# Row sums of x2 on VectorE ahead of the product with ones, and new orders of the later begin and of the end, in a four-layer conditioned residual block

## The reference

```python
# layer 0: a weight of rank 30 per entry, decoded from cond_512
U = (mu @ W_dec + b_dec).reshape(B, 257, 30); param = einsum('bik,kj->bij', U, V)
x = x + x @ param[:, :-1] + param[:, -1]
# layer 1: style-modulated product, demodulated, plus bias, clipped to +-256
x = x + clip(dcoef * ((x * style) @ weight) + bias, -256, 256)
# layer 2: down to 64 features, relu, up again, both conditioned on the entry
w_down = down_project * dg + db; w_up = up_project * ug + ub
x = x + relu(x @ w_down) @ w_up + x
# layer 3: layer norms with gains by token, three small nets on the conditions,
#          all weighted by softmax(aw), into a net 1536 -> 256 -> 256 with a last layer norm
x = x + _mlp_ln(concat([w0*h, w1*t, w2*m, w3*n, w4*r, w5*s]), int_W1, ..., int_g, int_be)
```

## Time and profile before

| | |
|---|---|
| median of 3 runs | 518.64 us (517.88, 518.64, 521.16) |
| span of the profiled execution | 518.5 us |
| the profiled execution's own time beside its span | none shown; the run nearest to the span is 518.64 |
| PE busy | 486.3 us (94%) |
| DVE busy | 410.5 us (79%) |
| ACT busy | 355.5 us (69%) |
| POOL busy | 406.9 us (78%) |
| mean granted TensorE clock | 0.985 |

### The profile page before, as it was taken

One profiled execution on the slowest core, in us unless ns is written; L12 is line 12 of the kernel. 1 busy time (PEld: TensorE's weight loads), 2 busy tenths in 40 slices (PEclk: granted clock), 3 DMA queues, 4 the chain that ended last, 5 costly groups with the idle time before them and its releaser, 6 DMA issues.

```text
span 518.5 us, 9615 instructions
## 1 busy us (share of the span) xinstructions
PE 486.3 (94%) x3216; PEld 361.9 (70%) x3245; DVE 410.5 (79%) x701; ACT 355.5 (69%) x666; POOL 406.9 (78%) x380
## 2 busy tenths in 40 slices
PE   8987788999999999999999999999999999988993
PEld 4854555677777686868686877777777767677782
DVE  4978697668788788788888888788888788887753
ACT  4677657558667677776878777777777776657732
POOL 6737798988798979798988888888989788786501
PEclk9999699999999999999999999999999999999997
DMA  8994507324234261708080817162534425113102
GB/s 294 336 335 98 127 1 219 82 82 127 83 89 120 60 189 36 212 21 226 0 236 11 214 33 195 53 176 72 139 110 118 133 54 148 53 40 125 41 2 80
DMA packets 35117, 61.82 MB, mean 119 GB/s; under 512 B 5107, under 2 KB 17541, under 8 KB 34708
## 3 DMA queue, kind: packets, MB, share of 16 engines
q1 hardware_dynamic: 28788, 44.01, 30.4%
q0 software_dynamic: 5440, 16.87, 11.0%
q10 hardware_dynamic: 864, 0.61, 0.4%
HBM read 52.61 MB, written 8.87 MB: 119 GB/s over the span
## 4 chain that ended last, share of the span: by engine, by line
PE 75%; ACT 7%; DVE 6%; issue 5%; POOL 5%; DMA 1%; DVEq 0%; ACTq 0%; POOLq 0%
PE ps_d L966 10%; PE ps_c L916 9%; PE ps_c L918 9%; PE ps_c L917 9%; PE ps_d L980 5%; PE ps_a L994 4%; PE ps_b L916 3%; PE ps_b L917 3%; PE ps_b L918 3%; PE ps_b L1012 3%; PE ps_a L1006 2%; POOL pw_rows L1532 2%; PE ps_a L1012 2%; DMA set_wdec<-in_W_dec 1%; PE ps_b L935 1%
## 5 line engine op out<-in xcount | busy, mean ns | idle before, releaser
L1232 ACT ACTIVATE h<-h,nb_h,rstd_h 128x256 f32<-128x256 f32 x64 | 33.3, 591 | 41.2 <-POOL nb_h L1562 41.2
L966 PE MATMUL ps_d<-xm_t,l_w 128*128 128x512 f32 x128 | 59.8, 610 | 1.7 <-DVE h L1455 0.9
L1532 POOL DMA_INDIRECT pw_rows<-in_pw,gidx x40 | 39.0, 976 | 12.2 <-issue 12.2
L1577 POOL TENSOR_TENSOR h<-xhat,pw_rows 128x1024 f32<-128x1024 f32 x16 | 38.0, 2374 | 6.4 <-ACT xhat L1232 6.4
L966 PEld LDWEIGHTS ps_d<-xm_t,l_w 128*128 128x128 f32 x128 | 23.6, 194 | 26.7 <-issue 24.5
L1596 POOL TENSOR_TENSOR w_up<-up_rep,ugub 128x1024 f32<-128x1024 f32 x16 | 38.1, 2378 | 2.9 <-DMA ugub<-ugub_scratch 1.9
L1598 POOL TENSOR_TENSOR w_up<-w_up,ugub 128x1024 f32<-128x1024 f32 x16 | 39.3, 2456 | 1.3
L1582 POOL TENSOR_TENSOR h<-h,pw_rows 128x1024 f32<-128x1024 f32 x16 | 38.3, 2396 | 1.2
L994 PE MATMUL ps_a<-act_dn,w_up 128*128 128x128 f32 x256 | 33.4, 286 | 5.3 <-ACT act_dn L1211 4.7
L1608 POOL TENSOR_TENSOR x3be<-x,ln_gb 128x1024 f32<-128x1024 f32 x16 | 37.9, 2372 | 0.3 <-DVE y_out L1513 0.3
L916 PE MATMUL ps_b<-w_h,act_t_l 128*128 128x256 f32 x128 | 37.7, 295 | 0.4 <-DVE act_t_l L1477 0.4
(11 more groups left out here) (263 smaller groups left out, 1607.9 us busy)
## 6 DMA issues: line engine op xcount, KB each, us to landing
ugub<-ugub_scratch SPq DMA_DIRECT2D x32, 512.0 KB, 6.6
x_t<-in_x_t SPq DMA_DIRECT2D x16, 512.0 KB, 6.5
out<-y_out SPq DMA_DIRECT2D x15, 512.0 KB, 7.2
set_wdec<-in_W_dec SPq DMA_DIRECT2D x2, 1920.0 KB, 9.6
set_wdec<-in_int_W SPq DMA_DIRECT2D x1, 1536.0 KB, 11.1
set_wdec<-in_nets_rows SPq DMA_DIRECT2D x1, 1152.0 KB, 15.5
set_wdec<-in_nets_W SPq DMA_DIRECT2D x1, 768.0 KB, 6.5
pw_rows<-in_pw,gidx POOLq DMA_INDIRECT x40, 3.6
```

The source lines that it names most:

```text
L966: m = eng.matmul(ps_l1[:, o, :], l1_w[:, k, o * P:(o + 1) * P], xm_t[:, k, :], start=k == 0, stop=k == KB - 1)
L1232: m = eng.activation(out[:, j, :], src[:, j, :], ACT.Identity, bias=nb[k][:, j:j + 1], scale=rstd[k][:, j:j + 1])
L1532: eng.indirect_dma_start(pw_rows[:, j, :], None, t["pw"], bass.IndirectOffsetOnAxis(ap=idx[:, j:j + 1], axis=0)).then_inc(s_pw[c.ring], 16)
L1577: eng.tensor_tensor(h1[:, :, :], xhat[:, :, :], pw_rows[:, :, 0:D], ALU.mult).then_inc(g_h1m, 1)
```

## The change

A tile x2_sum (128 x 512 float32) and a VectorE stage `v_xsum` are added. `v_xsum` adds the two feature halves of x2, right after `v_x2add` in each list, for all 16 chunks. `pe_dn` takes part 0 from x2 as before (four matmuls) and part 1 from x2_sum with one half of the ones (two matmuls instead of four), after a wait for `v_xsum`. The loop's orders stay as they are, with `v_xsum` put in. The semaphore d_aw is merged into d_bias (load_aw moves ahead of load_side, and the waits for d_bias become 32), and `act_onehot` waits for its own previous one-hot. The lists of the later begin and of the end are written anew on each engine.

```diff
@@ pe_dn
             x = x2_t[c.ring][:, :, :].rearrange("p k (j e s) -> p k e j s", e=2, s=S)
-            for part in range(2):
-                for k in range(KB):
-                    for e in range(2):
-                        m = eng.matmul(ps_dn[e * HID:(e + 1) * HID, part * CT * S:(part + 1) * CT * S],
-                                       down_w[:, k, part * HID:(part + 1) * HID], x[:, k, e],
-                                       start=k == 0, stop=k == KB - 1)
+            for k in range(KB):
+                for e in range(2):
+                    eng.matmul(ps_dn[e * HID:(e + 1) * HID, 0:CT * S], down_w[:, k, 0:HID], x[:, k, e],
+                               start=k == 0, stop=k == KB - 1)
+            wait(eng, v_xs, c.n + 1)
+            x = x2_sum[:, :].rearrange("p (j e s) -> p e j s", e=2, s=S)
+            for e in range(2):
+                m = eng.matmul(ps_dn[e * HID:(e + 1) * HID, CT * S:2 * CT * S], down_w[:, 0, HID:P], x[:, e],
+                               start=True, stop=True)
             m.then_inc(p_dn, 1)
@@ act_onehot
             wait(eng, s_idx[c.ring], 32 * (c.half + 1))
+            wait(eng, a_oh, c.n)
@@
+        def v_xsum(eng, c):
+
+            if first(c):
+                eng.wait_ge(d_ug, 16)
+            wait(eng, v_x2, c.n + 1)
+            wait(eng, p_dn, c.n)
+            eng.tensor_tensor(x2_sum[:, :], x2_t[c.ring][:, 0, :], x2_t[c.ring][:, 1, :], ALU.add).then_inc(v_xs, 1)
@@ TensorE, begin
-                             (pe_dn, 0), (pe_t, 2), (pe_warm, 2), (pe_up, 0), (pe_x3r, 0), (pe_l1, 1),
-                             (pe_x1, 2), (pe_mot, 0), (pe_xht, 0), (pe_cls, 0), (pe_dn, 1), (pe_row, 0),
-                             (pe_t, 3), (pe_cp, 0), (pe_up, 1), (pe_warm, 3), (pe_warm, 4), (pe_x3r, 1),
+                             (pe_t, 1), (pe_hid, 0), (pe_l1, 0), (pe_mo, 0), (pe_x1, 1), (pe_dn, 0), (pe_t, 2),
+                             (pe_warm, 2), (pe_up, 0), (pe_l1, 1), (pe_x3r, 0), (pe_mot, 0), (pe_x1, 2), (pe_cls, 0),
+                             (pe_xht, 0), (pe_dn, 1), (pe_row, 0), (pe_t, 3), (pe_up, 1), (pe_cp, 0), (pe_warm, 3),
...
@@ ScalarE, begin
-                             (act_w1scale, 0), (act_u, 2), (act_onehot, 0), (act_relu, 0), (act_w1high, 0),
-                             (act_th1, 2), (act_th2, 2), (act_x3, 0), (act_onehot, 1), (act_xnorm, 0),
-                             (act_mot, 0), (act_u, 3), (act_xht, 0), (act_x3h, 0), (act_th1, 3), (act_relu, 1),
-                             (act_shift, 0), (act_hnorm, 0), (act_rowwrite, 0), (act_hh, 0), (act_th2, 3),
+                             (act_onehot, 0), (act_u, 3), (act_relu, 0), (act_onehot, 1), (act_th1, 2),
+                             (act_w1high, 0), (act_th2, 2), (act_x3, 0), (act_mot, 0), (act_xnorm, 0), (act_xht, 0),
+                             (act_x3h, 0), (act_relu, 1), (act_shift, 0), (act_hnorm, 0), (act_th1, 3),
...
@@ VectorE, begin
-                             (v_x2add, 0), (v_x1add, 1), (v_w1sum, 0), (v_dnmul, 0), (v_dnadd, 0),
-                             (v_mostat, 0), (v_x3sum, 0), (v_xstat, 0), (v_monorm, 0), (v_l1mul, 1),
+                             (v_l1mul, 0), (v_l1min, 0), (v_x2add, 0), (v_xsum, 0), (v_x1add, 1), (v_dnmul, 0),
+                             (v_mostat, 0), (v_dnadd, 0), (v_w1sum, 0), (v_x3sum, 0), (v_monorm, 0), (v_xstat, 0),
...
@@ VectorE, loop: the one difference
+                             (v_x2add, 3), (v_xsum, 3), (v_hlow, 5), (v_tmprod, 5), (v_dnmul, 3), (v_dnadd, 3),
...
@@ GpSimd, begin
-                             (g_dcoef, 0), (g_tlow, 1), (g_wup, 0), (g_style, 1), (g_moroot, 0), (g_w1tlow, 0),
-                             (g_tlow, 2), (g_w1xlow, 0), (g_rootx, 0), (g_w2low, 0), (g_w1mlow, 0), (g_hmul, 0),
-                             (g_hadd, 0), (g_wup, 1), (g_rooth, 0), (g_style, 2), (g_gather, 1), (g_res, 0),
+                             (g_dcoef, 0), (g_tlow, 1), (g_wup, 0), (g_w2low, 0), (g_style, 1), (g_moroot, 0),
+                             (g_wup, 1), (g_w1mlow, 0), (g_tlow, 2), (g_rootx, 0), (g_w1tlow, 0), (g_hmul, 0),
+                             (g_hadd, 0), (g_w1xlow, 0), (g_style, 2), (g_rooth, 0), (g_gather, 1), (g_res, 0),
...
@@ GpSimd, end
-                      end=[(g_wup, 13), (g_hmul, 12), (g_hadd, 12), (g_tlow, 14), (g_rooty, 10), (g_gather, 13),
-                           (g_rooth, 12), (g_res, 12), (g_style, 14), (g_rootx, 13), (g_wup, 14), (g_hmul, 13),
-                           (g_hadd, 13), (g_rooty, 11), (g_tlow, 15), (g_rooth, 13), (g_gather, 14),
+                      end=[(g_wup, 13), (g_hmul, 12), (g_hadd, 12), (g_tlow, 14), (g_rooty, 10), (g_res, 12),
+                           (g_rooth, 12), (g_style, 14), (g_gather, 13), (g_rootx, 13), (g_wup, 14), (g_hmul, 13),
+                           (g_hadd, 13), (g_tlow, 15), (g_rooty, 11), (g_rooth, 13), (g_gather, 14), (g_style, 15),
...
```

More of the change, by code:

```diff
@@ L274, in conditioned_residuals @@
         x2_t = x1_t
-        (d_front, d_bdec, d_aw, d_side, d_bias, d_l1, d_wts, d_id, d_net, d_w2n, d_rown, d_w1, d_late, d_oh, d_gain, d_cls,
+        x2_sum = late("x2_sum", [P, CH])
+        (d_front, d_bdec, d_side, d_bias, d_l1, d_wts, d_id, d_net, d_w2n, d_rown, d_w1, d_late, d_oh, d_gain, d_cls,
          d_ub, d_ug, d_row) = (
             sem("d_" + n) for n in
-            "front bdec aw side bias l1 wts id net w2n rown w1 late oh gain cls ub ug row".split())
+            "front bdec side bias l1 wts id net w2n rown w1 late oh gain cls ub ug row".split())
         d_dec = [sem(f"d_dec{n}") for n in range(KB)]
@@ L430, in load_aw @@
         def load_aw(eng, c):
-            eng.dma_start(aw[:, :], row(t["aw"]).broadcast_to([P, 6])).then_inc(d_aw, 16)
+            eng.dma_start(aw[:, :], row(t["aw"]).broadcast_to([P, 6])).then_inc(d_bias, 16)
         def load_side(eng, c):
@@ L608, in v_awmax @@
         def v_awmax(eng, c):
-            eng.wait_ge(d_aw, 16)
+            eng.wait_ge(d_bias, 32)
             v_link(eng.reduce_max(aw_c[0][:, :], aw[:, :], AX.X))
@@ L728, in act_style @@
             eng.wait_ge(m_st, 1)
-            eng.wait_ge(d_bias, 16)
+            eng.wait_ge(d_bias, 32)
             for o in range(KB):
@@ new lines, in _ @@
+                             (act_rowwrite, 0), (act_hh, 0), (act_x3, 1), (act_xnorm, 1), (act_th2, 3), (act_tmh, 0),
+                             (act_relu, 2), (act_gidx, 3), (act_msh, 0), (act_xht, 1), (act_x3h, 1), (act_u, 4),
+                             (act_hnorm, 1), (act_silu, 0), (act_silh, 0), (act_th1, 4), (act_x3, 2), (act_hh, 1),
+                             (act_xnorm, 2), (act_th2, 4), (act_tmh, 1), (act_relu, 3), (act_ysquare, 0),
+                             (act_msh, 1), (act_xht, 2), (act_onehot, 2), (act_x3h, 2)],
@@ new lines, in _ @@
+                             (v_l1mul, 0), (v_l1min, 0), (v_x2add, 0), (v_xsum, 0), (v_x1add, 1), (v_dnmul, 0),
+                             (v_mostat, 0), (v_dnadd, 0), (v_w1sum, 0), (v_x3sum, 0), (v_monorm, 0), (v_xstat, 0),
+                             (v_l1mul, 1), (v_l1min, 1), (v_x1add, 2), (v_x2add, 1), (v_xsum, 1), (v_classes, 0),
+                             (v_dnmul, 1), (v_dnadd, 1), (v_hstat, 0), (v_x3low, 0), (v_rows, 0), (v_x3sum, 1),
+                             (v_hprod, 0), (v_xstat, 1), (v_hlow, 0), (v_l1mul, 2), (v_l1min, 2), (v_x2add, 2),
@@ new lines, in _ @@
+                             (v_xsum, 2), (v_tmprod, 0), (v_dnmul, 2), (v_dnadd, 2), (v_tmlow, 0), (v_msprod, 0),
+                             (v_hstat, 1), (v_mslow, 0), (v_x3low, 1), (v_x3sum, 2)],
+                      order=[(v_x1add, 3), (v_hprod, 5), (v_xstat, 4), (v_sillow, 6), (v_l1mul, 3), (v_l1min, 3),
+                             (v_x2add, 3), (v_xsum, 3), (v_hlow, 5), (v_tmprod, 5), (v_dnmul, 3), (v_dnadd, 3),
+                             (v_tmlow, 5), (v_msprod, 5), (v_ygain, 6), (v_mslow, 5), (v_hstat, 4), (v_ynorm, 6),
+                             (v_x3low, 4), (v_x3sum, 3)],
```

160 lines of the change are left out of this document (69 added, 91 removed).

## The result

The changed kernel takes 525.71 us (median; 523.85 to 527.31) against 519.9 for the kernel before on the same chip: a ratio of 1.0113, with a 95% interval of 1.0077 to 1.015. It is slower by 1.1%. The profiled execution of it took 527.31 us at a span of 525.5, so its time lies 1.8 above its span. It is the slowest of the four runs: its mean granted clock is 0.978, theirs 0.981 to 0.984. The sum of the prediction set the span of 518.5 equal to a time, and so began about 1.5 us too low.

What follows compares the result with a forecast made beforehand. TensorE's own queue was taken to bound the loop. From 518.5 us, +4.8 for the sum, -2.0 for the begin and -2.3 for the end gave 519.0 us, with a range of 511.0 to 524.5.

Steps and rivals of the forecast that it cites:

- The bound of the loop: Loop: TensorE's own instructions set the 27.2 us period; v_hlow ends 1.0 us before pe_w2, all the room there is.
- Removed from TensorE: pe_dn: four matmuls fewer, 0.47 us per chunk, 7.5 us over 16 chunks if all of it counted.
- Added to VectorE: v_xsum in the loop: held until GpSimd's running w_up ends, plus 0.55; about 1.2 us instead of 0.69.
- What is queued behind it: Loop: v_hlow ends late, so pe_w2 does too; period 0.4 us longer, +4.8 us over 12 chunks.
- The begin and the end of the sum: v_xsum outside the loop: 0.69 us in the begin; 0.4 us for each of the end's first two chunks.
- The orders: New lists of begin and end: -2.0 us in the later begin, -2.3 us in the end.
- rival of the held clock: Begin: a shorter TensorE gap keeps the 2.4 GHz level, 2.7 us less, 516.3 us; chance 0.10.
- pe_l1(1) ahead of it: Begin: pe_l1(1) before pe_x3r(0) makes chunk 0 late, +3.0 instead of -2.0, 524.0 us; chance 0.17.
- a sum that nothing blocks: Loop: VectorE and GpSimd don't exclude each other, or GpSimd's phase slips clear; pe_w2 0.13 early, 512.6 us; chance 0.10.
- The full saving: Loop: all of the 0.47 us arrives because pe_w2 does not meet v_hlow's end, 508.6 us; chance 0.08.
- GpSimd keeping its turn: Loop: v_xsum waits for GpSimd's next instruction (L1577) too, +2.6 us in 12 chunks, 545 us; chance 0.04.

Runs made afterwards that it cites:

- e8: The changed kernel without v_xsum, with the short pe_dn: the ones product reads x2's first feature half alone; 513.42 us.
- e3: The changed kernel with one input of v_xsum taken from PSUM (ps_l1) and not from SBUF; 514.53 us.
- e12: The changed kernel with the sum and short pe_dn in the loop's ten chunks alone; 0.63% or 3.3 us above the new orders without the sum.
- e14: The changed kernel with the sum and short pe_dn in chunks 0 to 2 alone; 2.3 us above the new orders without the sum.
- e15: The changed kernel with the sum and short pe_dn in chunks 13 to 15 alone; 2.7 us above the new orders without the sum.
- e2: The changed kernel without v_xsum and with the old eight-matmul pe_dn, so the new orders alone; 515.6 us.
- e9: The changed kernel with v_xsum run but unused: pe_dn has its old eight matmuls and no wait for the sum; 522.94 us.
- e4: The changed kernel with GpSimd's second w_up instruction (128x1024) cut into four of 128x256; 525.31 us.

## Why the prediction was wrong

**The bound of the loop: right.** TensorE's queue, 1.0 us from v_hlow.

**Removed from TensorE: right in size.** e8 shows 0.43 of the 0.47.

**Added to VectorE: right for the loop.** The exclusion, its end 0.55 behind the running instruction and the cause (e3) held. I forecast v_xsum at about 1.2 us; it took 1.18 and 1.29.

**What is queued behind it: right.** I took +0.4 a period, from 27.2 to "near 27.6"; it is 0.32 to 0.33 (27.53 to 27.54). For the 12 chunks of that pattern that is 3.9 instead of 4.8, and e12 measured 3.3 us for ten of them.

**The begin and the end of the sum: this step failed.** The sum was priced at 0.69 in the begin ("v_xsum (0.69) and v_mostat (52.53 to 54.88, 2.35) in front"), and the end had 0.4 for each of its first two chunks and nothing for the last. The row from which I took the rule, 1.88 and 2.72 us for L685 and L686, was itself from the begin and said what a sum costs that meets a GpSimd instruction just begun. I used it for the loop's phase alone ("the ten chunks of the loop and the first two of the end"), where 0.65 us of the instruction were left. Six sums outside the loop stand in other phases: 1.94, 1.00 and 2.79 us in the begin and 1.37, 2.68 and 0.69 in the end. By e14 and e15 they cost 2.3 and 2.7 us, and on top of the loop's ten 6.7 (changed kernel against e12). In the profiled execution TensorE stood 1.74 and 1.31 us for two of them, and behind each wait its clock fell and took 1.5 us more, a term that my sum didn't have. The range should have held 16 sums, each between 0.69 and 2.95 us (2.4 and 0.55).

**The orders: the size right, half of the causes wrong.** I took -2.0 and -2.3, 4.3 together; the spans of e2 and the kernel before differ by 4.3 and the ratios by 0.79%, 4.1 us. The halves are 1.3 in the begin and 3.0 in the end, by the traces. In the begin pe_up(0) takes 2.02 us at 53.10 in e2 (3.75 at 53.62 before): the clock stayed at its upper level behind a gap of 2.15 us instead of 3.34, which was my rival of the held clock. pe_x3r(0) still starts at 58.43 (58.77 before), so pe_l1(1) ahead of it cost nothing and its rival was wrong. Nor did it gain: in the changed kernel pe_up(0) stands at 53.47 and not near 52, behind a wait of 0.87 us for the sum of chunk 0, and pe_x3r(0) at 58.76. In the end the gather of chunk 13 and tlow(15) gave nothing that a row shows: from pe_dn(13) to pe_dn(15) e2 takes 55.40 us and the kernel before 55.59. The gain came from gather(15), of which I had written that "the very tail of chunk 15 isn't touched".

**The tail's gap.** In the changed kernel TensorE stands 2.85 us before L1030, and its matmuls then come 0.43 us apart for some 3 us, the 1.2 GHz level; in e2 the same gap is 1.63 and they come 0.22 to 0.24 apart, the 2.4 GHz level. pe_w2(14) starts 25.15 us behind pe_w2(13) there, 22.36 in e2 and 22.29 in e9. GpSimd's h(15) stood 4.10 us there and 3.03 in e2. The profile names no releaser; of what its code waits for, the gather's landing is what is left. Why it landed later wasn't tried, so these 2.8 us have a place and no cause. They are not shown to be the sum's: e3, whose sum nothing blocks, and e8, which has none, stand 2.41 and 2.51 us in the same place at the lower clock behind it, and their pe_w2(14) starts 24.73 and 25.08 us behind pe_w2(13).

Of the rivals, a sum that nothing blocks was to give 512.6: e3 is that case at 514.53. The full saving was 508.6: e8 is that case at 513.42, the rest given back in the end. GpSimd keeping its turn never happened. The time of 525.7 is the forecast's mechanism with the base 1.5 too low, the loop 0.9 too dear, and a remainder of some 6 us, which falls on the sums outside the loop (6.7 by e12).

## What to carry to other kernels

Price an added instruction in every phase in which it runs, not in the steady one alone: with three chunks before the loop and three behind it, the six outside cost 5.0 us alone and 6.7 on top of the ten inside, which cost 3.3. A wait of TensorE can cost more than its length: here 1.5 us more where the clock fell behind it. A VectorE operation on two SBUF operands beside long GpSimd instructions has no one duration but a span, from its own to that plus most of a GpSimd instruction; give it one operand from PSUM where that can be had, or leave it out. And split a change that mixes an edit with new orders: here the orders alone, 515.6 us, beat both kernels by 0.8 and 1.9%, and hid 4 of the 10 to 11 us that the edit costs.

## What the runs showed of the hardware that I had not expected

The end of the blocked sum is the firmest number of the case: 0.54 to 0.56 us behind the end of the running GpSimd instruction, at the begin, in the loop and in the end, and the GpSimd instruction behind it is 0.3 to 0.45 us longer (2.69 against 2.39 for w_up, 2.83 against 2.38 for the product behind it). Four GpSimd instructions of 128x256 in a row took 3.25 us with a VectorE sum let in between them, where one of 128x1024 took 2.39. The length of TensorE's gap alone didn't say what its clock did: it stayed at its upper level behind gaps of 1.32, 1.63, 1.75 and 2.15 us (e15, e2's tail, e14, e2's begin) and fell to its lower one behind 1.31 and 1.74 as well as 2.85 (all in the changed kernel) and 3.34 us. So the 2.4 us in my expectation for e15 was no limit. No run varied the gap by itself. And the time of a run lies 1.7 to 1.9 us above its span in every kernel here but e4, where it is 2.0.
